# GNN block kernel: a 128-target window for each edge chunk, and the second message layer at the end of the loop body

## What is computed

```python
# layer 0: messages, summed at their source
m = jnp.concatenate([x[row], x[col]], axis=1)
m = relu(m @ Wm1 + bm1)
m = relu(m @ Wm2 + bm2)
m_sum = segment_sum(m, row, num_segments=N)
# layer 1: graph attention over the edges (needs how often an edge src -> dst occurs)
# layer 2: mean over the first 10 edges of each source
keep = rank < 10
# layer 3: weighted sum
agg = segment_sum(edge_weight[:, None] * x[src], dst, num_segments=N)
```

## Time and profile before

| | |
|---|---|
| median of 3 runs | 899.65 us (896.03 to 900.72) |
| the profiled execution, its own time | 891.63 us |
| its span | 889.8 us |
| mean granted TensorE clock | 0.988 |
| busy: PE, DVE, ACT, POOL | 831.1, 676.1, 489.0, 301.7 us |
| edge loop | 137 to 504 us of the span |

### The profile page before, as it was taken

The page is one execution under the profiler, slowest core; times in us unless marked ns, Lnnn a source line. Parts: engine busy times, 40 slices in busy tenths (PEclk is TensorE's granted clock), DMA queues, the critical chain, the costliest instruction groups (busy, mean ns, idle before and its releaser), DMA issues.

```text
span 889.8 us, 18629 instructions
## 1 busy us (share of the span) xinstructions
PE 831.1 (93%) x5465; PEld 535.1 (60%) x5466; DVE 676.1 (76%) x1800; ACT 489.0 (55%) x995; POOL 301.7 (34%) x403
## 2 busy tenths in 40 slices
PE   8899968999999999999999999899999998999898
PEld 3657727989898989898989856422242223322244
DVE  6899985777676777776767756899869986999650
ACT  6432104666656666666666665466655675566521
POOL 8140047556555556565555400011231120032000
PEclk9999978999999999999999999999999999999999
DMA  3120032121212121222122200000000000000400
GB/s 89 34 89 0 1 136 66 47 71 53 69 49 72 53 71 48 71 53 72 53 71 48 71 1 1 0 1 0 1 1 1 0 1 1 1 0 1 156 33 25
DMA packets 19146, 35.87 MB, mean 40 GB/s; under 512 B 5281, under 2 KB 11553, under 8 KB 18977
## 3 DMA queue, kind: packets, MB, share of 16 engines
q0 software_dynamic: 7104, 19.41, 7.8%
q1 hardware_dynamic: 12000, 15.95, 5.1%
HBM read 29.56 MB, written 5.79 MB: 40 GB/s over the span
## 4 chain that ended last, share of the span: by engine, by line
PE 72%; DVE 18%; ACT 4%; issue 3%; POOL 2%; DMA 0%; DVEq 0%; POOLq 0%; ACTq 0%
PE PS L1320 8%; DVE OHd L1016 7%; PE PS L1233 7%; PE PS L1234 7%; PE PS L1468 6%; PE PS L1314 6%; PE PS L1181 6%; PE PS L1252 5%; PE PS L1226 4%; PE PS L1459 3%; PE PS L1368 3%; PE PS L1239 3%; DVE PS L1027 3%; PE PS L1311 2%; PE PS L1453 2%
## 5 line engine op out<-in xcount | busy, mean ns | idle before, releaser
L409 POOL DMA_INDIRECT room<-Qtab,gidx x148 | 148.2, 1001 | 96.0 <-DVE gidx L842 61.1
L559 ACT ACTIVATE OHe<-OHs,sew 128x128 bf16<-128x128 bf16 x408 | 126.6, 389 | 40.6 <-DVE OHs L952 22.7
L1016 DVE CUSTOM_DVE_ANT_0 OHd<-PS,room 128x1024 bf16<-128x1024 f32 x96 | 112.8, 1220 | 10.2 <-PE PS L1419 10.1
L423 POOL TENSOR_SCALAR KV<-room,pid 128x256 bf16<-128x256 uint8 x74 | 74.2, 1004 | 130.2 <-DVE MS L917 125.1
L570 ACT ACTIVATE m2s<-m2s 128x512 f32<-128x512 f32 x68 | 42.8, 630 | 90.6 <-DVE m2s L943 47.0
L461 POOL TENSOR_TENSOR zl<-AL,Sx 128x8 f32<-128x8 f32 x9 | 7.6, 840 | 234.6 <-DVE Sx L1016 234.6
L1233 PE MATMUL PS<-Wm,m1T 128*128 128x256 f32 x276 | 83.2, 383 | 0.0
L1234 PE MATMUL PS<-Wm,m1T 128*128 128x256 f32 x276 | 83.0, 383 | 0.0
L943 DVE TENSOR_TENSOR m2s<-PS,bm 128x512 f32<-128x512 f32 x68 | 47.0, 690 | 44.8 <-PE PS L1234 44.8
L957 DVE TENSOR_SCALAR OHd<-iotaN,dstf 128x1024 bf16<-128x1024 f16 x136 | 74.0, 584 | 9.0 <-PE PS L1320 8.7
L1320 PE MATMUL PS<-OHs,m2s 128*128 128x128 f32 x544 | 76.6, 284 | 0.1
(11 more groups left out here) (360 smaller groups left out, 1669.7 us busy)
## 6 DMA issues: line engine op xcount, KB each, us to landing
BT<-Wtab SPq DMA_DIRECT2D x1, 4096.0 KB, 14.1
room<-Qtab,gidx POOLq DMA_INDIRECT x148
room<-Stab SPq DMA_DIRECT2D x1, 2048.0 KB
Wtab<-H SPq DMA_DIRECT2D x4, 512.0 KB, 3.4
Wtab<-cs SPq DMA_DIRECT2D x4, 512.0 KB, 3.4
Qtab<-room SPq DMA_DIRECT2D x1, 1024.0 KB, 4.5
Wn<-in_L_gnn_Wn SPq DMA_DIRECT2D x1, 1024.0 KB, 5.6
x<-in_x SPq DMA_DIRECT2D x1, 512.0 KB, 4.3
```

The source lines that it names most:

```text
L409: g.indirect_dma_start(out=G[:, p % SLOTS, k, :], out_offset=None, in_=Qtab, in_offset=bass.IndirectOffsetOnAxis(ap=gidx[:, p, k:k + 1], a ...
L423: g.tensor_scalar(OHsT[:, p % SLOTS, :], srow[:, min(p, NPAIR - 1) * PAIR:][:, 0:PAIR], pid1[:], None, ALU.is_equal)\
L559: a.activation(OHe[:, k, j, :], OHs[:, k, :], ACT.Copy, scale=sew[:, j, bass.ds(2 * g + k, 1)])
L1016: v.tensor_tensor_reduce(junk[n % 2], bank(4, 2), mask[:, i, :], 1.0, 2 * FAR, ALU.subtract, ALU.max, Sx[:, i, hd:hd + 1]).then_inc(S("gat ...
```

## The change

Three things change. **The window of targets:** a pair no longer walks blocks of 256 targets for both chunks. Each chunk has a window of 128 targets of its own, which begins at a multiple of 32 and does not cross target 512 (PSUM banks hold 512 columns); a pass then has 8 matmuls where it had 16. If a chunk's targets don't fit in such a window, the pair is wide and walks blocks of 128 targets with both chunks, one block a pass. **The setup** that finds the windows is another: the largest and the smallest target of each chunk by transposes and reductions, and 19 small VectorE instructions; TensorE transposes their result to one row before its first `sources`. **The order in the body:** the transposes of the next message move from the end of the body to its head, behind the register load, and the second layer alone ends the body. One wait at L992 is written in another form.

```diff
-            v.tensor_copy(paired(dstf), sdst)
-            link(v.tensor_scalar(paired(skey), sdst, 7, None, ALU.arith_shift_right))
-            link(v.tensor_copy(sew0[:], skey[:]))
-            link(v.scalar_tensor_tensor(rngp[:], sew0[:], 1.0, valid[:], ALU.add, ALU.mult))
-            v.tensor_tensor(inblk, rngp[:].unsqueeze(1).to_broadcast([P, NB, NCH]),
-                            iota[:, 1:NB + 1].unsqueeze(2).to_broadcast([P, NB, NCH]), ALU.is_equal)\
+            link(v.tensor_copy(paired(dstf), sdst))
+            v.scalar_tensor_tensor(rngp[:], dstf[:], 1.0, valid[:], ALU.add, ALU.mult)
+            v.scalar_tensor_tensor(sew0[:], dstf[:], float(-N), valid[:], ALU.add, ALU.mult)\
...
+            v.tensor_reduce(above[:], ends[:, 0], AX.X, ALU.max)
+            v.tensor_reduce(below[:], ends[:, 1], AX.X, ALU.min).then_inc(S("ends_read"), 1)
+            link(v.tensor_scalar(least[:], below[:], float(N), float(N - 1), ALU.add, ALU.min))
+            v.tensor_scalar(steps[:], least[:], 5, None, ALU.arith_shift_right)
+            link(v.tensor_scalar(upper[:], least[:], 9, None, ALU.arith_shift_right))
+            link(v.tensor_scalar(other[:], upper[:], float(BANK // STEP), float((BANK - P) // STEP), ALU.mult, ALU.add))
+            link(v.tensor_tensor(place[:], steps[:], other[:], ALU.min))
+            link(v.scalar_tensor_tensor(other[:], place[:], float(-STEP), above[:], ALU.mult, ALU.add))
+            link(v.tensor_tensor(wide[:], other[:, 0:1], other[:, 1:2], ALU.max))
+            v.tensor_scalar(wide[:], wide[:], float(P), None, ALU.is_gt)
...
+            eng.wait_ge(S("packed"), 1)
+            t.transpose(bank(4)[0:1, 0:NPAIR], packed[:], ident[0:NPAIR, 0:NPAIR]).then_inc(S("packed_across"), 1)
...
-            layers(0)
+            eng.wait_ge(S("m1_ready"), 1)
+            second_layer(0)
+            second_layer(1).then_inc(S("m2_done"), 1)
...
                 with eng.Fori(g0, end) as g:
-                    eng.wait_ge(S("spans"), 1)
-                    span = eng.value_load(rngi[0:1, bass.ds(g, 1)], min_val=1, max_val=NB * NB * NB - 1)
...
+                    near = eng.snap((span << 2) & (N - STEP))
+                    past = eng.snap(near + ((span & (NB - 1)) << 7) + P)
+                    further = eng.snap(((span >> 3) & (N - STEP)) - near)
+                    eng.wait_ge(S("msg_ready"), g + 2)
+                    transposes()
...
-                    with eng.Fori(least, past, 2) as d:
+                    with eng.Fori(near, past, P) as d:
                         for k in range(2):
-                            for i in range(2):
-                                at = d * P + i * P
-                                dst = OHd[:, k, bass.ds(at, P)]
-                                t.matmul(PS[:, bass.ds(at, P)], OHc[:, k, :], dst,
+                            at = nc.s_assert_within(d if k == 0 else d + further, 0, N - P,
+                                                    skip_runtime_bounds_check_because="windows lie inside the nodes")
+                            dst = OHd[:, k, bass.ds(at, P)]
+                            t.matmul(PS[:, bass.ds(at, P)], OHc[:, k, :], dst,
+                                     start=False, stop=False, skip_group_check=True)
+                            for j in range(3):
+                                t.matmul(PS[:, bass.ds(at + 2 * BANK, P)], OHe[:, k, j, :], dst,
                                          start=False, stop=False, skip_group_check=True)
...
-                    layers(g + 1)
+                    eng.wait_ge(S("m1_ready"), g + 2)
+                    second_layer(0)
+                    second_layer(1).then_inc(S("m2_done"), 1)
```

More of the change, by code:

```diff
@@ L41 @@
 HALF = 65536.0
+STEP = 32
+PLACES = N // STEP
 FAR = -1e30
@@ L159, in gnn_kernel @@
         FEW = 32
[L160 to L165, removed]
+        above = sb("above", [NPAIR, 2])
+        below = sb("below", [NPAIR, 2])
+        least = sb("least", [NPAIR, 2], i32)
+        steps = sb("steps", [NPAIR, 2], i32)
+        upper = sb("upper", [NPAIR, 2], i32)
+        place = sb("place", [NPAIR, 2])
+        other = sb("other", [NPAIR, 2])
+        wide = sb("wide", [NPAIR, 1])
+        packed = sb("packed", [NPAIR, 1])
+        rngi = sb("rngi", [1, NPAIR], i32)
         Wn1 = sb("Wn1", [P, 4, 4 * D])
@@ L873, in _ @@
             made = bank(5).rearrange("p (k f) -> p k f", k=2)
[L874 to L886, removed]
+            eng.wait_ge(S("ends_across"), 1)
@@ new lines, in _ @@
+            link(v.tensor_scalar(upper[:, 1:2], upper[:, 0:1], 7, None, ALU.arith_shift_right))
+            link(v.tensor_tensor(above[:, 0:1], above[:, 0:1], above[:, 1:2], ALU.max))
+            link(v.scalar_tensor_tensor(above[:, 1:2], upper[:, 1:2], float(-P), above[:, 0:1], ALU.mult, ALU.add))
+            link(v.tensor_scalar(steps[:, 0:1], above[:, 1:2], float(P - 1), None, ALU.add))
+            link(v.tensor_scalar(steps[:, 1:2], steps[:, 0:1], 7, None, ALU.arith_shift_right))
+            v.scalar_tensor_tensor(below[:, 0:1], steps[:, 1:2], -1.0, wide[:], ALU.add, ALU.mult)
@@ new lines, in _ @@
+            link(v.scalar_tensor_tensor(other[:], upper[:, 1:2].to_broadcast([NPAIR, 2]), float(P // STEP), place[:],
+                                        ALU.mult, ALU.subtract))
+            link(v.scalar_tensor_tensor(place[:], other[:], wide[:, 0:1], place[:], ALU.mult, ALU.add))
+            link(v.scalar_tensor_tensor(below[:, 1:2], place[:, 1:2], float(PLACES), place[:, 0:1], ALU.mult, ALU.add))
+            v.scalar_tensor_tensor(packed[:], below[:, 1:2], float(NB), below[:, 0:1], ALU.mult, ALU.add)\
+                .then_inc(S("packed"), 1)
@@ L1257, in _ @@
             eng.wait_ge(S("sources_across"), 1)
-            eng.wait_ge(S("blocks_marked"), 1)
-            for u in range(2):
-                marks = inblk[:, u * NB // 2:(u + 1) * NB // 2, :].rearrange("p b (g k) -> p b g k", k=2)
+            eng.wait_ge(S("ends_marked"), 1)
+            for u, end in enumerate((rngp, sew0)):
                 for k in range(2):
-                    last = t.matmul(bank(6 + u)[0:FEW, 0:NB // 2 * NPAIR], onesb[:, 0:FEW], marks[:, :, :, k],
-                                    start=(k == 0), stop=(k == 1))
-            last.then_inc(S("blocks_counted"), 1)
+                    at = (2 * u + k) * P
+                    last = t.transpose(bank(6)[0:NPAIR, at:at + P], paired(end)[:, :, k], ident[:])
+            last.then_inc(S("ends_across"), 1)
             t.sem_inc(S("pair_done"), 1)
```

44 lines of the change are left out of this document (12 added, 32 removed).

## The result

The changed kernel takes 903.64 us (median of 7 runs, 900.23 to 906.06) where the kernel before takes 898.56 (7 runs, 896.03 to 900.72): a ratio of 1.0046, 95% interval 1.0027 to 1.0066 (the quotient of the two medians is 1.0057). It is slower by about half a per cent: 905 was forecast, and the difference is clear of the noise, though about as small as the 0.5% under which the forecast called it none. Its profiled execution took 900.23 us.

A forecast was written before the change was run, and what follows sets the result against it. GpSimd's gather chain was taken to bound pairs at 5.06 us. Terms 0 + 7.4 - 1.5 - 0.3 = +5.6 us took the profiled 891.63 to 897.2; with 8.0 from profile to median, 905 us, range 893 to 912.

The forecast's parts named there:

- Chain 3: GpSimd in the loop: message sum to second gather's end 4.26 us, next message sum 0.80 behind; claimed to bound at 5.06.
- chain 1: TensorE's own matmuls in a pair: 5.04 us before, 4.59 after the change; bounding every pair there had chance 0.04.
- chain 4: TensorE's sequencer, twice round the loop: 9.89 us for two pairs, 4.95 each, unchanged by the edit.
- chain 3 is no wait: Rival: the message sum's 0.5 us follows something other than the gather; pairs bound at 4.95, time 900; chance 0.19.
- VectorE's chain: Rival: ordinary pairs fall to the loop through VectorE and TensorE, 4.81 us; change -5.6 us, time 894; chance 0.11.
- The ordinary pair stays as it is: Ordinary loop pairs still take 5.06 us and TensorE idles where the matmuls were: 0.
- Passes: Loop passes go from 71 to 77: nine second passes at 1.2 us come, three at 1.12 go, +7.4 us.
- the second pass is hidden: Rival: with enough work queued at TensorE, an extra pass costs only its matmuls, 0.45 us; time 898.5; chance 0.09.
- From block to block: At seven block changes the transposes fit ahead of the ranks: 0, at most 7 x 0.2 us either way.
- Setup: Before the loop: packed row near 130.3, first sources 130.5, second layer of first pair near 135.0; -1.5 us, between -3 and +1.
- End: Behind the loop: 0.44 us less behind the last ranks, the start then bound by L961: -0.3 us.
- The head: Rival: transposes and ranks right behind the register load show 0.15 us in each ordinary pair, +6.8, time 912; chance 0.13.

The follow-up runs named there:

- the first experiment: Changed kernel with GpSimd issuing both gathers of a round ahead of the turned one-hots, from the fifth round on: 893.24 us, ratio to before 0.9933.
- side by side: Before, order alone and changed kernel, none with a new edit, profiled once each on one chip: 894.84, 897.08 and 897.51 us.
- experiment eight: Changed kernel with no pair marked wide, so each pair makes one pass, 68 in all, output not the reference's: 889.09 us, ratio 0.9942.
- the order alone: Kernel before, with its passes and setup, only the transposes moved to the body's head and the second layer alone at its end: 896.51 us, ratio 0.9977.
- windows alone: Changed kernel with its windows and setup, but the transposes back at the end of the body as before: 904.32 us, ratio 1.0065.
- the later start: Changed kernel with gathers ahead of the turned one-hots, begun some 0.3 us later by waiting for the sources' next one-hots: 891.79 us, ratio 0.9961.
- experiments two to five and eight to eleven: Windows alone 904.32 us; order alone 896.51; changed plus two semaphore updates 904.12; before again 894.21; one pass each 889.09; unedited changed 897.51, before 894.84, order alone 897.08.

## Why the prediction was right, and where only its sum was

**What bounds the pair.** Right, and the doubt is gone. Chain 3 was read from two pairs of before; moved away from the end of the sources, the same gathers let the pair fall to 5.00 in before (chain 1, summed to 5.04) and to 4.96 and 4.92 in the changed kernel (chain 4, 4.95). So chains 1 and 3 were there within 0.04 us of the price at which they were read, and that is why half the matmuls of the target loop were worth nothing; of chain 4 only the number is confirmed. The rival "chain 3 is no wait" is refuted; its time of 900 needed 4.95 in the changed kernel, which came only with the first experiment. The rivals with 4.81 (VectorE's chain) and 4.59 (chain 1) in every pair are refuted too: the shortest ordinary interval in the changed kernel's first profile is 5.08.

**The ordinary pair stays as it is.** Nearly: the term was 0. On one chip it was +0.01 to +0.03 in each of 44 pairs, about 1 us, and between the two first profiles +0.08, 3.4 us. The step that was mis-sized is "chain 3 has none of the edited parts and stays 5.06": the lag behind the gather was 0.04 longer in the two kernels with the transposes at the head, and another 0.05 from one profile to another.

**Passes.** Right in number (77) and nearly in size. From the first two profiles: seven wide pairs at 6.24 and one at 7.58 over 5.15 make 7 x 1.09 + 2.43 = 10.1, less 3 x 1.13 = 3.4, so +6.7; side by side 7 x 1.17 + 2.61 - 3 x 1.19 = +7.2. The sum had +7.4. A pass is 1.20 us from first matmul to first matmul, as costed, and a pair then pays 1.09 to 1.17 of it in the mean. (Among its signs the forecast lists eight intervals of about 6.3; by its own count of passes it is seven, and seven came.) The rival "the second pass is hidden" (0.45) is refuted by the same rows and by experiment eight.

**From block to block.** The seven changes of block and the pairs behind them add up to 86.9 us before and 87.6 after: +0.8, inside the bound of 1.4 that went with the 0.

**Setup.** The term was -1.5 and should have been -4.1 (143.08 to 139.00) or -4.8 (143.71 to 138.92), beyond even its bound of -3. The step that failed is "the packed row is there near 130.3 and the first sources start at 130.5". VectorE was free for the first reduction at 122.77 instead of 124.4, two reductions took 0.41 each instead of 1.0 in all, and the 19 small instructions ran from 123.55 to 126.83, 0.17 each, not 0.26: on one or two columns they are shorter than on 72. So the row was packed 2.2 us ahead of the first sources, which went on waiting for GpSimd (129.01, has 129.19). The second layer then began at 133.49 where I had 135.0 and before had 136.58.

That is 3.1 of the 4.1 us. Most of the rest is a thing that the forecast left out, the granted clock. It is 0.50 (1.2 GHz) until 141.05 in before and until 135.28 in the changed kernel, and 1.00 (2.4 GHz) from there on. So all of before's second layer runs at the lower level (136.58 to 139.99, where the ranks follow, 3.41 us), and the last part of the changed kernel's at the higher (133.49 to 136.11, 2.62 us):

```profile
139.14 1.06 PE L1234 MATMUL PS<-Wm,m1T 128*128 128x256 f32 x2
...
135.68 0.59 PE L1234 MATMUL PS<-Wm,m1T 128*128 128x256 f32 x2
```

The first line is before's, the second the changed kernel's. The order seems to bring most of the gain: side by side it is 12.1 us from the setup's first message sum to the loop's first in before, 9.1 with the order alone and 9.2 in the changed kernel.

**End.** The first matmul behind the loop (L1350, at 513.34) follows the last message sum by 3.35 us, before by 3.55 (506.18 in the earlier trace rows less 502.63): -0.2, with -0.3 forecast.

So the sum was +5.6 and the medians moved by +5.1, but by two errors that cancel in part: a setup gain 2.6 to 3.3 us too small and ordinary pairs 1 to 3.4 us too cheap. The base had an error too, 899.65 from three runs where seven gave 898.56. That 905 came so close to 903.64 is owed to them and is luck. That the freed array time is worth nothing and the windows lose is not: windows alone gave 1.0065, and one pass each 0.9942.

**The head.** I gave 0.15 a pair to the rival that transposes and ranks at the head would show. A fourth of that may be there (0.04 of lag, from one profile each), by a way that I had not thought of, and not as an idle array.

**Versions that beat both.** Gathers ahead of the one-hots: 0.9933 in the changed kernel, 0.9958 in before, 0.9944 in before with the new order, 0.9961 with the later start. Their intervals overlap, so I don't rank them; each is faster than the change and lies 0.4 to 0.7% under before. What they share is that GpSimd issues its gathers ahead of the one-hots.

## What to carry to other kernels

When two chains close within 0.02 us, taking work from one is worth nothing until the other is known; price every chain up to the next kernel's bound before costing the edit. An extra turn of this dynamic loop cost its sequencer's instructions and not its matmuls: 1.19 us with 0.90 of matmuls, 1.20 with 0.45. So a smaller tile that needs more turns must be counted in turns. And look where an indirect gather ends: here TensorE's completions came late in the half microsecond behind it, and moving the gather was worth more than taking work away.

## What the runs showed of the hardware

A completion of TensorE that falls just behind the recorded end of a round's second gather reaches its waiter late. These are the 680 message sums of the loop in ten profiles (before and changed, and experiments two to five and eight to eleven), each set against the gather that ended last before it:

| sources end, against the gather's recorded end | message sums | message sum comes |
|---|---|---|
| 0.07 us or more ahead | 8 | 0.30 behind the sources in seven, 0.78 in one |
| 0.13 behind | 1 | 0.61 behind the gather, 0.49 behind the sources |
| 0.18 to 0.59 behind | 469 | 0.75 to 0.96 behind the gather |
| 0.72 or more behind | 202 | 0.30 behind the sources |

It is TensorE's semaphore update that is late. In before it is recorded 0.46 to 0.62 us behind the gather's end wherever it is held, and in the changed kernel 0.58 to 0.64 in 43 of 44, wherever in that stretch the sources ended; otherwise it is 0.01 behind the matmul. It holds for other lines as well: in the changed kernel six updates of the second layer (L1234), eight of the ranks (L1239) and eight of the transposes (L1226) are recorded 0.44 to 0.64 behind a second gather. Updates of VectorE and ScalarE in the same stretch are recorded 0.01 behind their ends, as anywhere else. And not every gather does it: behind the first gather of a round 50 completions of L1234 fall 0.19 to 0.55 us after its end in the changed kernel, and their updates are recorded 0.01 behind the matmuls.

The Trainium skill (Perfetto Trace Analysis, DMA Instruction — SWDGE (GPSIMD)) says that the end recorded for such an instruction is when the last descriptor has been generated, not when the transfer is over. By that, the held half microsecond may still be the gather's own work; no run here shows what is done in it. The ends of matmuls in a trace are modelled, so it is also open whether the update alone is late or the matmuls behind it end later than drawn. Nor does a run show why the lag is 0.81 in before and 0.84 to 0.90 with the windows, the new order or both. That stays open.
